# Skip term written into the accumulator bank, products in whole runs, and the third adding transfer one step later, in a fused Mamba, cross-attention and FFN kernel

## The chip, the cores and the metric

The kernel runs on one core of a Trainium2 chip. A core has a matrix engine (TensorE, PE in the tables; its weight loads are listed as PEld), a vector engine (VectorE, DVE), an activation engine (ScalarE, ACT), a general engine (GpSimd, POOL), a queue engine that issues transfers (SyncE, SP), 16 DMA engines, an on-chip memory of 128 partitions (SBUF) and eight accumulator banks (PSUM). The metric is the time of one execution in microseconds on the device.

## What is computed

Three residual blocks, each followed by a layer norm. Only the first is touched by the change.

```python
def _mamba(x, W_in, W_conv, b_conv, W_xproj, W_dt, b_dt, A_log, D, W_out):   # x: (8, 512, 512)
    xr = x @ W_in.T
    xc, res = (xr[..., :DI], xr[..., DI:])                     # DI = 1024
    u = silu(conv4(transpose(xc)) + b_conv)                    # causal, 4 taps, per channel
    x_dbl = jnp.einsum('bdl,ed->ble', u, W_xproj)              # -> dt (32), B (16), C (16)
    delta = jax.nn.softplus(dt @ W_dt.T + b_dt)
    A = -jnp.exp(A_log)
    dA = jnp.exp(jnp.einsum('bld,dn->lbdn', delta, A))         # 16 states per channel
    dBu = jnp.einsum('bld,bln,bdl->lbdn', delta, B, u)
    # h = dA_t * h + dBu_t ;  y_t = sum over the 16 states of h * C_t
    y = jnp.transpose(ys, (1, 2, 0)) + u * D[None, :, None]    # the skip term is u * D
    y = jnp.transpose(y, (0, 2, 1)) * silu(res)
    return y @ W_out.T

x = _layernorm(x + _mamba(x, ...))
x = _layernorm(x + cross_attention(x, ctx, ...))
x = _layernorm(x + ffn(x, ...))
```

## The kernel before

Two passes run one after the other. The first, `mamba_pass`, takes the first residual block; the second, `cross_attention_ffn_pass`, takes the other two and is the same text before and after.

The first pass walks over 64 blocks: 8 batches (b) times 8 groups of 128 channels (d). Below, g = 8b + d is the number of a block. In a block there are 8 steps, k = 0 to 7, each for two of the 16 states and all 512 time steps; q = 8g + k numbers the steps. Every engine has its own instruction stream, written out in program order as a loop over `step(b, d, k)`, and the streams meet only in semaphores. What each does in a step:

- PE, `b_products(q + 1)` (L381): sixteen small fp32 matmul instructions that make delta·u·B of the next step in one of two pairs of banks. It waits until the scan of step q − 1 has read the pair (`scanned`), so PE is at most two steps ahead of DVE.
- DVE, `scan` (L789): two scans, one per state, which turn the decays in a slot of a 12-slot ring into the states. Between scans it does the convolution taps (`conv_tap`, L765) of the next batch's u, the gating of y (`gate_y`, L797), and residual adds with layer norm statistics (`add_first`, L804; `add_second`, L811 to L816).
- ACT, `decay` (L635): two exponentials, which fill a ring slot some steps ahead of the scan. It waits until the slot's old content has been consumed. Between decays it takes results out of banks (`last_tap` L598, `take_vt` L619, `take_res` L643, `take_yt` L654) and computes silu and softplus, with a table load whenever the function set changes.
- POOL, `times_c` (L898): multiplies the states of a step by C. Three times a block it issues an adding transfer `merge(g, p)` (L907) of 1024 KB, which adds two ring slots onto the next two, so that after the third one only two slots of the block hold all the sums. Each of the three waits for the one before to have landed (`merged`).

In step k = 6 of the next block PE turns the two slots around into y's bank, adding them up (`state_sum`, L402). In between, four transposing matmuls (`skip_transposes`, L411) add u·D, which ACT had put into the buffer `y_t` in step k = 2 (`scale_skip`, L649). In step k = 7 ACT copies the bank into `y_t` (`take_yt`) and PE transposes it back into the same bank (`y_transposes`, L417), where DVE gates it.

The wide products, matmuls with 512 columns, stand between these in PE's stream. There are four families: `u_product` (L296, the convolution's input for the next batch), `x_product` (L306), `res_product` (L349), `out_first` and `out_second` (L436 and L444, the output projection). An fp32 product over one tile is two matmul instructions in the trace. A hand-written table says how many tiles of which product come in which step; most steps hold two tiles, which is half a `u_product` or `res_product`.

SP issues the loads. In the last block of a batch it fetches the next batch's rows of C (`mamba_c_row`, four times 1024 KB), B's diagonals (`mamba_diag_b`, eight times 256 KB) and an input tile (`mamba_xt`, 1024 KB).

Of the kernel before, what the change touches and what calls it, by code (L numbers as in the profile page):

```python
# [10 lines left out]
P = 128  # L11
# [3 lines left out]
def mamba_pass(nc, x, x_t, c_dram, diag_dram, w_u, w_res, w_conv, b_conv, w_x, w_dt, a_log, d_skip, w_out, ident_d, x1):  # L15
# [3 lines left out]
    KT = DM // P  # L19
# [24 lines left out]
    with ctx:  # L44
# [235 lines left out]
        def _(pe):  # L280
# [127 lines left out]
            def skip_transposes(g):  # L408
# [40 lines left out]
            def step(b, d, k):  # L449
# [25 lines left out]
                if d in (0, 4):  # L475
                    if k == 3:
                        res_product(g, [0, 1])
                    if k == 7:
                        res_product(g, [2, 3])
                if d in (1, 5, 7):  # L480
                    if k == 2:
                        res_product(g, [0, 1])
                    if k == 3:
                        res_product(g, [2, 3])
                if d in (2, 3):
                    if k == 3:
                        res_product(g, [0, 1])
                    if k == 4:
# [1166 lines left out]
```

## Time and profile before

| | |
|---|---|
| median of three runs | 2563.59 us |
| lowest, highest | 2558.22, 2564.44 us |
| the profiled execution's own time | 2562.99 us |
| its span, first to last instruction | 2561.2 us |
| mean granted TensorE clock, share of full speed | 0.973 |
| PE, PEld busy | 94%, 55% of the span |
| DVE, ACT, POOL busy | 71%, 58%, 65% of the span |

Busy shares are means over both passes. The first pass ends at about 1706 us of the span; the questions of this change are all asked there. A row of a timeline merges like instructions that follow each other and gives the start of the first; the difference between the starts of two rows of one engine is what the first cost, which is a little less than the busy time in the row, since instructions overlap at their ends. A bracket at the end of a row is idle time in front of it, and what ended it. "Issuing" a transfer on POOL has a row of its own.

### The profile page before, as it was taken

The page shows a single profiled execution, that of the slowest core. Times are in us where ns is not written, and L with a number is a line of the kernel's source. Part 1 is how long each engine was busy: PE and PEld are TensorE (multiplying, and loading weights), DVE is VectorE, ACT ScalarE, POOL GpSimd, SP SyncE. Part 2 cuts the span into 40 slices and gives each one's busy share as a digit, 9 for nine tenths or more (in the row PEclk, how much of TensorE's full clock was granted, in tenths as well). Part 3 has the DMA queues.
Part 4 walks back from the last instruction along what each step waited for, and adds up shares of the span by engine and source line. Part 5 has one row for each costly group of instructions (what it writes and reads, how often), then busy time and mean ns, then how long its engine had stood idle before and what let it go on. Part 6 is the DMA issues. An engine that isn't in the chain of part 4 may idle for free. (4 is left out here: it accounts for less than half of the span.)

```text
span 2561.2 us, 38451 instructions
## 1 busy us (share of the span) xinstructions
PE 2395.1 (94%) x15488; PEld 1418.2 (55%) x15488; DVE 1829.3 (71%) x2154; ACT 1473.8 (58%) x2258; POOL 1668.6 (65%) x912
## 2 busy tenths in 40 slices
PE   7899999999999999999999988877999999999997
PEld 3566566656665666656656656653545455454543
DVE  2898798798798789789879879841364565466453
ACT  2586678678678668768766867731333343443332
POOL 0698899798898889889978989860331332234130
PEclk8899999999999999999999999988999999999998
DMA  3777978978977887897897797755000100010000
GB/s 126 201 163 163 236 162 173 241 162 177 230 169 167 206 207 161 182 235 161 170 245 154 165 227 154 164 119 211 1 1 34 33 11 23 34 34 1 17 17 17
DMA packets 158832, 342.75 MB, mean 134 GB/s; under 512 B 39232, under 2 KB 102208, under 8 KB 127808
## 3 DMA queue, kind: packets, MB, share of 16 engines
q0 software_dynamic: 27648, 201.34, 40.0%
q1 hardware_dynamic: 131008, 138.97, 16.5%
q8 instruction: 123, 2.02, 0.3%
q14 instruction: 53, 0.43, 0.1%
HBM read 119.57 MB, written 19.37 MB: 54 GB/s over the span
## 5 line engine op out<-in xcount | busy, mean ns | idle before, releaser
L898 POOL TENSOR_TENSOR mamba_ring<-mamba_ring,mamba_c_row 128x1024 f32<-128x1024 f32 x512 | 1278.3, 2631 | 63.1 <-DVE mamba_ring L789 60.9
L789 DVE TENSOR_TENSOR_SCAN mamba_ring<-mamba_ring,ps 128x512 f32<-128x512 f32 x1024 | 1180.4, 1203 | 190.8 <-PE ps L381 190.0
L635 ACT ACTIVATE mamba_ring<-mamba_delta,mamba_a_neg 128x512 f32<-128x512 f32 x1024 | 661.2, 711 | 111.0 <-DMA mamba_ring<-mamba_ring 109.7
L381 PEld LDWEIGHTS ps<-mamba_diag_b,mamba_v_t 64*128 64x128 f32 x8192 | 504.7, 189 | 320.9 <-issue 244.3
L381 PE MATMUL ps<-mamba_diag_b,mamba_v_t 64*128 64x128 f32 x8192 | 595.5, 286 | 34.3 <-DVE mamba_ring L789 33.5
L296 PE MATMUL ps<-mamba_xt,mamba_wu 128*128 128x512 f32 x512 | 254.5, 625 | 31.7 <-DMA mamba_xt<-x_t 16.1
L907 POOL DMA_DIRECT2D mamba_ring<-mamba_ring x192 | 179.6, 936 | 142.0 <-DMA mamba_ring<-mamba_ring 107.4
L1554 POOL TENSOR_TENSOR xf_pr<-xf_pr,xf_top 128x1232 f32<-128x1232 f32 x32 | 75.0, 2343 | 281.0 <-DVE xf_top L1472 281.0
L349 PE MATMUL ps<-mamba_xt,mamba_wres 128*128 128x512 f32 x512 | 256.6, 619 | 0.0
L402 PE MATMUL ps<-mamba_ident,mamba_ring 128*128 128x128 f32 x1024 | 145.2, 288 | 43.7 <-DMA mamba_ring<-mamba_ring 43.6
L765 DVE SCALAR_TENSOR_TENSOR mamba_u<-ps,mamba_wcv,mamba_u 128x511 f32<-128x511 f32 (+2 forms) x192 | 142.4, 741 | 54.6 <-ACT mamba_u L598 50.9
L436 PE MATMUL ps<-mamba_wout,mamba_u 128*128 128x512 f32 x352 | 175.3, 617 | 0.0
L1547 POOL TENSOR_TENSOR xf_xn<-xf_xn,xf_bo_s 128x512 f32<-128x512 f32 x32 | 39.5, 1266 | 204.5 <-PE xf_ps L1122 204.5
L296 PEld LDWEIGHTS ps<-mamba_xt,mamba_wu 128*128 128x128 f32 x512 | 90.3, 194 | 115.4 <-issue 96.8
L402 PEld LDWEIGHTS ps<-mamba_ident,mamba_ring 128*128 128x128 f32 x1024 | 121.1, 148 | 52.1 <-issue 46.2
L598 ACT ACTIVATE mamba_u<-ps,mamba_bcv,mamba_wcv 128x512 f32<-128x512 f32 x64 | 49.5, 773 | 155.4 <-PE ps L296 155.4
L1335 ACT ACTIVATE xf_pr<-xf_pr 128x1232 f32<-128x1232 f32 x32 | 39.3, 1230 | 168.7 <-POOL xf_pr L1554 168.7
L1513 DVE TENSOR_TENSOR xf_xn<-xf_xn,xf_ps 128x512 f32<-128x512 f32 x32 | 21.2, 662 | 158.3 <-PE xf_ps L1231 158.3
L890 POOL TENSOR_TENSOR mamba_v<-mamba_delta,mamba_u 128x512 f32<-128x512 f32 x64 | 98.1, 1533 | 45.2 <-ACT mamba_delta L615 44.3
L1361 ACT COPY xf_pt<-xf_ps 77x512 f32<-77x512 f32 x128 | 64.8, 587 | 103.0 <-PE xf_ps L1214 103.0
L349 PEld LDWEIGHTS ps<-mamba_xt,mamba_wres 128*128 128x128 f32 x512 | 85.5, 189 | 69.0 <-issue 53.5
L586 ACT ACT_TABLE_LOAD x95 | 121.9, 1283 | 1.7
(116 smaller groups left out, 2948.6 us busy)
## 6 DMA issues: line engine op xcount, KB each, us to landing
mamba_ring<-mamba_ring POOLq DMA_DIRECT2D x192, 1024.0 KB, 7.8
mamba_c_row<-c_rows SPq DMA_DIRECT2D x32, 1024.0 KB, 15.7
mamba_wu<-w_u SPq DMA_DIRECT2D x64, 256.0 KB, 3.5
mamba_wres<-w_res SPq DMA_DIRECT2D x64, 256.0 KB, 6.0
mamba_diag_b<-b_diagonals SPq DMA_DIRECT2D x56, 256.0 KB, 14.9
mamba_xt<-x_t SPq DMA_DIRECT2D x8, 1024.0 KB, 16.0
mamba_xres<-x SPq DMA_DIRECT2D x32, 256.0 KB, 8.7
x<-mamba_xres SPq DMA_DIRECT2D x32, 256.0 KB, 5.8
```

The costliest lines, as they stand in the source:

```text
L296: m = nc.tensor.matmul(ps[:, bank, :], wu[n % 2][:, kt, :], xt[b % 2][:, kt, :], start=(kt == 0), stop=(kt == KT - 1))
L349: m = nc.tensor.matmul(ps[:, BANK_B, :], wres[g % 2][:, kt, :], xt[b % 2][:, kt, :], start=(kt == 0), stop=(kt == KT - 1))
L381: m = nc.tensor.matmul(ps[:, 2 * s + i, tb * P:(tb + 1) * P], v_t[g % 2][i * H:(i + 1) * H, tb * P:(tb + 1) * P], diag_b[i * H:(i + 1) * H ...
L402: m = nc.tensor.matmul(ps[:, y_bank(g), tb * P:(tb + 1) * P], ring[:, r, i, tb * P:(tb + 1) * P], ident[:], is_transpose=True, start=(k == ...
L436: m = nc.tensor.matmul(ps[:, o1_bank(tb), :], u[b % 2][:, d, tb * P:(tb + 1) * P], wout[:, d, :], start=(d == 0), stop=(d == MOST[tb] - 1))
L586: nc.scalar.preload_act_table_set("natural_log_exp_and_others")
L635: a = nc.scalar.activation(ring[:, q % NR, i, :], delta[:, d % EARLY, :], ACT.Exp, scale=a_neg[:, d, 2 * k + i:2 * k + i + 1])
L765: nc.vector.scalar_tensor_tensor(u[b % 2][:, j, lag:], ps[:, bank, 0:T - lag], wcv[:, j, TP - lag:TAPS - lag], u[b % 2][:, j, lag:], ALU.m ...
L789: m = nc.vector.tensor_tensor_scan(ring[:, r, i, :], ring[:, r, i, :], both[:, bass.ds(i, T, 2)], 0.0, ALU.mult, ALU.add)
L890: nc.gpsimd.tensor_tensor(v[:].rearrange("p b i t -> p i b t"), in_blocks(delta[:, d % EARLY, :]), in_blocks(u[b % 2][:, d, :]), ALU.mult) ...
L898: nc.gpsimd.tensor_tensor(ring[:, q % NR], ring[:, q % NR], c_row[:, 2 * k:2 * k + 2, :], ALU.mult).then_inc(c_done, 1)
L907: nc.gpsimd.dma_start(ring[:, dst:dst + 2], ring[:, src:src + 2], accum_op=ALU.add).then_inc(merged[p], 16)
```

## The change

Three things are done in the first pass.

First, the skip term goes another way. `skip_transposes` is gone from PE. ACT no longer writes u·D into `y_t` in step 2; in step 7, right after `take_yt` has copied y's bank out, it writes u·D into that same bank, and `y_transposes` adds onto it instead of overwriting. `y_transposes` now waits for both ACT instructions.

Second, wide products that stood in halves in neighbouring steps are put together, mostly four tiles in one step: `u_product` in steps 1 and 5, `res_product` in step 3 (5 where d = 6), `x_product` in steps 1 and 5 of d = 5, `out_first` and `out_second` in fewer, longer runs. Three residual adds on DVE move a step or two earlier with them.

Third, POOL issues the third adding transfer of a block behind the third `times_c` of the next block, where it stood behind the second.

```diff
+            def y_transposes(g):
+                pe.wait_ge(yt_ready, g + 1)
                 pe.wait_ge(du_ready, g + 1)
                 for tb in range(TT):
-                    nc.tensor.matmul(ps[:, y_bank(g), tb * P:(tb + 1) * P], y_t[:, tb * P:(tb + 1) * P], ident[:],
-                                     is_transpose=True, start=False, stop=False, skip_group_check=True)
-
-            def y_transposes(g):
-                pe.wait_ge(yt_ready, g + 1)
-                for tb in range(TT):
-                    m = nc.tensor.transpose(ps[:, y_bank(g), tb * P:(tb + 1) * P], y_t[:, tb * P:(tb + 1) * P],
-                                            ident[:])
+                    m = nc.tensor.matmul(ps[:, y_bank(g), tb * P:(tb + 1) * P], y_t[:, tb * P:(tb + 1) * P], ident[:],
+                                         is_transpose=True, start=False, stop=(tb == TT - 1), skip_group_check=True)
                 m.then_inc(y_back, 1)
...
                 if k == 6 and g >= 1:
-                    state_sum(g - 1, SUMS[0])
-                    skip_transposes(g - 1)
-                    state_sum(g - 1, SUMS[1])
+                    for e in SUMS:
+                        state_sum(g - 1, e)
...
-                    if k < 2:
-                        u_product(n, BANK_A, [2 * k, 2 * k + 1])
-                    if k in (4, 5) and d in TWO_U:
-                        u_product(n + 1, BANK_A, [2 * k - 8, 2 * k - 7])
+                    if k == 1:
+                        u_product(n, BANK_A, range(KT))
+                    if k == 5 and d in TWO_U:
+                        u_product(n + 1, BANK_A, range(KT))
...
-                    if k in (0, 1):
-                        x_product(b + 1, [2 * k, 2 * k + 1])
-                    if k in (4, 5):
-                        x_product(b + 1, [2 * k - 4, 2 * k - 3])
+                    if k in (1, 5):
+                        x_product(b + 1, range(k - 1, k + 3))
...
+                if k == (5 if d == 6 else 3):
+                    res_product(g, range(KT))
...
             def scale_skip(g):
                 b, d = g // ND, g % ND
+                act.wait_ge(yt_ready, g + 1)
+                nc.scalar.activation(ps[:, y_bank(g), :], u[b % 2][:, d, :], ACT.Copy,
+                                     scale=dsk[:, d:d + 1]).then_inc(du_ready, 1)
+
+            def take_yt(g):
+                act.wait_ge(summed, (g + 1) * NSUM)
                 if g >= 1:
                     act.wait_ge(y_back, g)
...
-                if k == 2 and g >= 1:
-                    scale_skip(g - 1)
                 if k == 7 and g >= 1:
                     take_yt(g - 1)
+                    scale_skip(g - 1)
...
-                if back and (d, k) == (3, 3):
+                if back and (d, k) == (3, 1):
                     add_second(b - 1, 2, y_bank(g - 1))
...
-                if (d, k) == (6, 4):
+                if (d, k) == (6, 3):
                     add_first(b, 0)
...
-                if (d, k) == (7, 5):
+                if (d, k) == (7, 3):
                     add_first(b, 2)
...
-                    if k == 1 and g >= 1:
+                    if k == 2 and g >= 1:
                         merge(g - 1, 2)
```

On PE, the front half of a block with d = 1 (from y's transposes of the block before to the small products of step 6), before. L296 is `u_product`, L349 `res_product`, L362 the transposes of v, L381 the small products of one step (x8 is one step here):

```order
L417 MATMUL ps<-mamba_ident,mamba_y_t 128x128 x4
L381 MATMUL ps<-mamba_diag_b,mamba_v_t 128x128 x8
L296 MATMUL ps<-mamba_xt,mamba_wu 128x512 x2
L381 MATMUL ps<-mamba_diag_b,mamba_v_t 128x128 x8
L296 MATMUL ps<-mamba_xt,mamba_wu 128x512 x2
L381 MATMUL ps<-mamba_diag_b,mamba_v_t 128x128 x8
L349 MATMUL ps<-mamba_xt,mamba_wres 128x512 x2
L381 MATMUL ps<-mamba_diag_b,mamba_v_t 128x128 x8
L349 MATMUL ps<-mamba_xt,mamba_wres 128x512 x2
L381 MATMUL ps<-mamba_diag_b,mamba_v_t 128x128 x8
L362 MATMUL ps<-mamba_ident,mamba_v 128x128 x4
L296 MATMUL ps<-mamba_xt,mamba_wu 128x512 x2
```

The same place after:

```order
L412 MATMUL ps<-mamba_ident,mamba_y_t 128x128 x4
L381 MATMUL ps<-mamba_diag_b,mamba_v_t 128x128 x16
L296 MATMUL ps<-mamba_xt,mamba_wu 128x512 x4
L381 MATMUL ps<-mamba_diag_b,mamba_v_t 128x128 x16
L349 MATMUL ps<-mamba_xt,mamba_wres 128x512 x4
L381 MATMUL ps<-mamba_diag_b,mamba_v_t 128x128 x8
L362 MATMUL ps<-mamba_ident,mamba_v 128x128 x4
L381 MATMUL ps<-mamba_diag_b,mamba_v_t 128x128 x8
L296 MATMUL ps<-mamba_xt,mamba_wu 128x512 x4
```

Where every step held two tiles, the small products of two steps now stand together and then come four tiles at once.

On ACT, from a block's `take_yt` to the u product's last tap in step 2 of the next block (d = 1), before. L649 is the skip term, L635 the decays, L643 the gate, L604 silu, L598 the last tap:

```order
L654 COPY mamba_y_t<-ps 128x512
L635 ACTIVATE mamba_ring<-mamba_delta,mamba_a_neg 128x512 x2
L643 ACT_TABLE_LOAD
L643 ACTIVATE mamba_gate<-ps 128x512
L604 ACTIVATE mamba_u<-mamba_u 128x512
L586 ACT_TABLE_LOAD
L635 ACTIVATE mamba_ring<-mamba_delta,mamba_a_neg 128x512 x4
L649 ACTIVATE mamba_y_t<-mamba_u,mamba_dsk 128x512
L598 ACTIVATE mamba_u<-ps,mamba_bcv,mamba_wcv 128x512
```

The same place after:

```order
L614 COPY mamba_y_t<-ps 128x512
L607 ACTIVATE ps<-mamba_u,mamba_dsk 128x512
L594 ACTIVATE mamba_ring<-mamba_delta,mamba_a_neg 128x512 x2
L602 ACT_TABLE_LOAD
L602 ACTIVATE mamba_gate<-ps 128x512
L563 ACTIVATE mamba_u<-mamba_u 128x512
L545 ACT_TABLE_LOAD
L594 ACTIVATE mamba_ring<-mamba_delta,mamba_a_neg 128x512 x4
L557 ACTIVATE mamba_u<-ps,mamba_bcv,mamba_wcv 128x512
```

The skip term has moved from in front of the last tap to right behind the copy out of y's bank, for which PE's last transposes of the block wait.

On POOL, one block and the start of the next, before. L890 makes v, L898 is `times_c`, L907 an adding transfer:

```order
L890 TENSOR_TENSOR mamba_v<-mamba_delta,mamba_u 128x2x4x64
L898 TENSOR_TENSOR mamba_ring<-mamba_ring,mamba_c_row 128x1024 x2
L907 DMA mamba_ring<-mamba_ring 128x2048
L898 TENSOR_TENSOR mamba_ring<-mamba_ring,mamba_c_row 128x1024 x2
L907 DMA mamba_ring<-mamba_ring 128x2048
L898 TENSOR_TENSOR mamba_ring<-mamba_ring,mamba_c_row 128x1024 x3
L907 DMA mamba_ring<-mamba_ring 128x2048
L898 TENSOR_TENSOR mamba_ring<-mamba_ring,mamba_c_row 128x1024
```

The same place after:

```order
L849 TENSOR_TENSOR mamba_v<-mamba_delta,mamba_u 128x2x4x64
L857 TENSOR_TENSOR mamba_ring<-mamba_ring,mamba_c_row 128x1024 x3
L866 DMA mamba_ring<-mamba_ring 128x2048
L857 TENSOR_TENSOR mamba_ring<-mamba_ring,mamba_c_row 128x1024
L866 DMA mamba_ring<-mamba_ring 128x2048
L857 TENSOR_TENSOR mamba_ring<-mamba_ring,mamba_c_row 128x1024 x3
L866 DMA mamba_ring<-mamba_ring 128x2048
L857 TENSOR_TENSOR mamba_ring<-mamba_ring,mamba_c_row 128x1024
```

Between the block before's third transfer and this block's first there were two C products, and now there is one.

## Rows read from the trace of the kernel before

**Rows 1.** Windows: busy us of each engine, granted clock, DMA share, GB/s.

```profile
core 0: us, PE busy (x) PEld busy (x) DVE busy (x) ACT busy (x) POOL busy (x), PEclk, DMA share, GB/s
868.00:922.00 54.00, 51.26 (x377) 31.95 (x376) 43.83 (x43) 35.06 (x51) 42.12 (x24) 1.00 1.02 266
...
900.00:1100.00 200.00, 195.27 (x1492) 123.34 (x1488) 174.12 (x179) 149.04 (x223) 173.67 (x94) 1.00 0.83 187
```

**Rows 2.** Timeline of PE, batch 4, blocks d = 0 to 2.

```profile
893.66 0.60 PE L417 MATMUL ps<-mamba_ident,mamba_y_t 128*128 128x128 f32 x4
...
896.52 1.98 PE L296 MATMUL ps<-mamba_xt,mamba_wu 128*128 128x512 f32 x4 [1.16 <-DMA mamba_xt<-x_t]
...
922.02 1.16 PE L381 MATMUL ps<-mamba_diag_b,mamba_v_t 64*128 64x128 f32 x16
923.11 1.98 PE L296 MATMUL ps<-mamba_xt,mamba_wu 128*128 128x512 f32 x4
925.02 1.16 PE L381 MATMUL ps<-mamba_diag_b,mamba_v_t 64*128 64x128 f32 x16
...
942.47 0.60 PE L411 MATMUL ps<-mamba_ident,mamba_y_t 128*128 128x128 f32 x4
942.90 1.04 PE L402 MATMUL ps<-mamba_ident,mamba_ring 128*128 128x128 f32 x8
...
962.90 2.84 PE L444 MATMUL ps<-mamba_wout,mamba_u 128*128 128x512 f32 x6
965.67 1.16 PE L381 MATMUL ps<-mamba_diag_b,mamba_v_t 64*128 64x128 f32 x16
...
1098.33 0.60 PE L417 MATMUL ps<-mamba_ident,mamba_y_t 128*128 128x128 f32 x4
```

**Rows 3.** Timeline of PE around waits: batches 4, 6, 2 and 7.

```profile
916.27 1.06 PE L402 MATMUL ps<-mamba_ident,mamba_ring 128*128 128x128 f32 x8 [1.57 <-DMA mamba_ring<-mamba_ring]
...
918.58 1.16 PE L381 MATMUL ps<-mamba_diag_b,mamba_v_t 64*128 64x128 f32 x16
...
1326.63 1.94 PE L402 MATMUL ps<-mamba_ident,mamba_ring 128*128 128x128 f32 x8 [2.67 <-DMA mamba_ring<-mamba_ring]
...
1330.50 1.16 PE L381 MATMUL ps<-mamba_diag_b,mamba_v_t 64*128 64x128 f32 x16
...
577.26 1.16 PE L381 MATMUL ps<-mamba_diag_b,mamba_v_t 64*128 64x128 f32 x16 [1.85 <-DVE mamba_ring L789]
...
1538.84 2.06 PE L381 MATMUL ps<-mamba_diag_b,mamba_v_t 64*128 64x128 f32 x32
```

**Rows 4.** Timeline of POOL, batch 4, blocks d = 0 and 1.

```profile
905.27 0.88 POOL L907 DMA_DIRECT2D mamba_ring<-mamba_ring  x1 [3.81 <-DMA mamba_ring<-mamba_ring]
905.88 4.97 POOL L898 TENSOR_TENSOR mamba_ring<-mamba_ring,mamba_c_row 128x1024 f32<-128x1024 f32 x2
911.15 0.88 POOL L907 DMA_DIRECT2D mamba_ring<-mamba_ring  x1 [0.30 <-POOL mamba_ring L898]
911.75 7.28 POOL L898 TENSOR_TENSOR mamba_ring<-mamba_ring,mamba_c_row 128x1024 f32<-128x1024 f32 x3
921.91 0.88 POOL L907 DMA_DIRECT2D mamba_ring<-mamba_ring  x1 [2.88 <-DMA mamba_ring<-mamba_ring]
922.52 2.66 POOL L898 TENSOR_TENSOR mamba_ring<-mamba_ring,mamba_c_row 128x1024 f32<-128x1024 f32 x1
924.84 1.57 POOL L890 TENSOR_TENSOR mamba_v<-mamba_delta,mamba_u 128x512 f32<-128x512 f32 x1
926.07 4.96 POOL L898 TENSOR_TENSOR mamba_ring<-mamba_ring,mamba_c_row 128x1024 f32<-128x1024 f32 x2
930.70 1.17 POOL L907 DMA_DIRECT2D mamba_ring<-mamba_ring  x1
```

**Rows 5.** Transfers: queue 0 over the span; L907 in 868 to 922; in 925 to 1040.

```profile
q0 software_dynamic: 27648, 201.34, 40.0%
...
mamba_ring<-mamba_ring POOLq DMA_DIRECT2D x6, 1024.0 KB, 11.2
...
mamba_ring<-mamba_ring POOLq DMA_DIRECT2D x14, 1024.0 KB, 7.6
```

**Rows 6.** Timeline of ACT: the hand-over of y, and the skip term.

```profile
918.69 0.58 ACT L654 COPY mamba_y_t<-ps 128x512 f32<-128x512 f32 x1
...
926.70 0.71 ACT L649 ACTIVATE mamba_y_t<-mamba_u,mamba_dsk 128x512 f32<-128x512 f32 x1
```

**Rows 7.** Timeline of DVE: three steps' scans in a row; two taps and the next scan.

```profile
903.22 1.53 DVE L765 SCALAR_TENSOR_TENSOR mamba_u<-ps,mamba_wcv,mamba_u 128x511 f32<-128x511 f32 x2 [0.38 <-ACT mamba_u L598]
904.67 2.32 DVE L789 TENSOR_TENSOR_SCAN mamba_ring<-mamba_ring,ps 128x512 f32<-128x512 f32 x2
...
907.55 6.76 DVE L789 TENSOR_TENSOR_SCAN mamba_ring<-mamba_ring,ps 128x512 f32<-128x512 f32 x6
```

More of the change, by code:

```diff
@@ L406, in state_sum @@
                 m.then_inc(summed, 1)
-            def skip_transposes(g):
+            def y_transposes(g):
+                pe.wait_ge(yt_ready, g + 1)
                 pe.wait_ge(du_ready, g + 1)
                 for tb in range(TT):
-                    nc.tensor.matmul(ps[:, y_bank(g), tb * P:(tb + 1) * P], y_t[:, tb * P:(tb + 1) * P], ident[:],
-                                     is_transpose=True, start=False, stop=False, skip_group_check=True)
-            def y_transposes(g):
-                pe.wait_ge(yt_ready, g + 1)
-                for tb in range(TT):
-                    m = nc.tensor.transpose(ps[:, y_bank(g), tb * P:(tb + 1) * P], y_t[:, tb * P:(tb + 1) * P],
-                                            ident[:])
+                    m = nc.tensor.matmul(ps[:, y_bank(g), tb * P:(tb + 1) * P], y_t[:, tb * P:(tb + 1) * P], ident[:],
+                                         is_transpose=True, start=False, stop=(tb == TT - 1), skip_group_check=True)
                 m.then_inc(y_back, 1)
@@ L500, in step @@
                 if d == 6:
-                    if k == 0:
-                        out_first(b, 0, [2, 3])
                     if k == 1:
-                        out_first(b, 1, [0, 1])
-                    if k == 2:
-                        out_first(b, 1, [2])
+                        out_first(b, 0, [2, 3, 4])
                     if k == 3:
-                        out_first(b, 0, [4])
-                        out_first(b, 1, [3])
-                    if k == 4:
-                        out_first(b, 1, [4])
+                        out_first(b, 1, [0, 1, 2, 3, 4])
+                    if k == 7:
+                        out_first(b, 2, [0, 1])
                 if d == 7:
-                    if k == 0:
-                        out_first(b, 2, [0, 1])
                     if k == 1:
-                        out_first(b, 2, [2, 3])
-                    if k == 4:
-                        out_first(b, 2, [4, 5])
+                        out_first(b, 2, [2, 3, 4, 5])
                     if k == 5:
-                        out_first(b, 3, [0, 1])
+                        out_first(b, 3, [0, 1, 2, 3])
                     if k == 7:
-                        out_first(b, 3, [2, 3, 4])
+                        out_first(b, 3, [4])
                 if back and (d, k) == (0, 0):
@@ L533, in step @@
                     dt_pair(b, 2)
-                if back and (d, k) == (1, 6):
+                if back and (d, k) == (1, 7):
                     pe.wait_ge(vt_ready, g + 2)
-                    out_second(b - 1, 0, y_bank(g), [5])
-                if back and (d, k) == (1, 7):
-                    out_second(b - 1, 0, y_bank(g), [6, 7])
+                    out_second(b - 1, 0, y_bank(g), [5, 6, 7])
                 if back and (d, k) == (2, 5):
@@ L545, in step @@
                     out_second(b - 1, 1, BANK_A, [5, 6, 7])
-                if back and (d, k) == (3, 2):
+                if back and (d, k) == (3, 0):
                     pe.wait_ge(vt_ready, g + 1)
@@ L574, in _ @@
                         step(b, d, k)
-            state_sum(NG - 1, SUMS[0])
-            skip_transposes(NG - 1)
-            state_sum(NG - 1, SUMS[1])
+            for k in SUMS:
+                state_sum(NG - 1, k)
             y_transposes(NG - 1)
@@ L646, in scale_skip @@
                 b, d = g // ND, g % ND
-                if g >= 1:
-                    act.wait_ge(y_back, g)
-                nc.scalar.activation(y_t[:], u[b % 2][:, d, :], ACT.Copy,
+                act.wait_ge(yt_ready, g + 1)
+                nc.scalar.activation(ps[:, y_bank(g), :], u[b % 2][:, d, :], ACT.Copy,
                                      scale=dsk[:, d:d + 1]).then_inc(du_ready, 1)
@@ L653, in take_yt @@
                 act.wait_ge(summed, (g + 1) * NSUM)
+                if g >= 1:
+                    act.wait_ge(y_back, g)
                 nc.scalar.copy(y_t[:], ps[:, y_bank(g), :]).then_inc(yt_ready, 1)
@@ L748, in _ @@
                         step(b, d, k)
+            take_yt(NG - 1)
             scale_skip(NG - 1)
-            take_yt(NG - 1)
             for tb in range(0, TT, 2):
```

22 lines of the change are left out of this document (removed).

## The prediction, made before the changed kernel had run

> **What bounds the kernel now.** I read four views in this order: the windows, the timeline of PE, the timeline of POOL, the transfers. The windows show the first pass: PE is busy for 195.27 of 200 us, DVE for 174.12, POOL's arithmetic for 173.67, and the DMA engines for 83% [rows 1]. So PE bounds it, but three others are close behind. At the turn from one batch to the next (868 to 922) the DMA engines are full, at 1.02 [rows 1].
>
> PE's timeline shows what filling it took. Step after step costs 3.0 us: the small products 1.09 (922.02 to 923.11), two tiles of a wide product 1.91 (923.11 to 925.02) [rows 2]. DVE's scans of a step cost 2.24 (6.76 for three, less 0.04 of overlap), and it can lag by at most two steps, so even steps of 3.0 leave room for taps in between. Batch 4 takes 204.67 us from y's transposes at 893.66 to the same at 1098.33, eight blocks [rows 2]; all of PE's idle gaps in it sum to 5.9 us, of which the two large kinds are a wait for the input tile (1.16) [rows 2] and one for an adding transfer (1.57) [rows 3]. PE's work per batch is then 204.7 − 5.9 = 198.8 us. The second pass does not change.
>
> I make the sum per batch, against batch 4, which has no stretch of low clock, and carry it to 2562.99 us, the profiled execution's own time. That stands 0.6 us below the median of the three runs, nothing beside the terms.
>
> **What the change takes from PE.** (a) The skip transposes: four per block, 942.47 to 942.90, 0.43 us [rows 2], times 8 = 3.5 per batch. (b) Run ends. Six wide instructions take 2.77 (962.90 to 965.67), four take 1.91 [rows 2], so one costs 0.43 and every run carries 1.91 − 4 × 0.43 = 0.19, say 0.2, once. Counted in the two tables, a batch has 54 such runs before and 30 after: 24 × 0.2 = 4.8. (c) Small products of two steps side by side: a pair is busy for 2.06 [rows 3] where two apart take 1.09 + 1.16 = 2.25. With some 8 such pairs per batch free of waits I take 1.4. Together 9.7, PE's work falls to 189.1 us. The input tile's wait goes too, since the first `u_product` now stands one step later than the 1.16 us that it waited. That is the case for the change: if PE stayed busy it would be worth 7% of the pass.
>
> **What it adds: (A) y's hand-over.** Before, two tiles or more stood between the sums and `y_transposes`. Now, in d = 0, 2, 3 and 4, only the small products of one step do, 1.09 us. In that time ACT must start (0.11 after the sums end: 918.58 to 918.69), copy (0.58) and write the skip term (0.71) [rows 3, 6], and the next engine must notice, 0.1: 1.5 us. PE waits 0.4. Where a second u product stands in step 5 (d = 0 and 4), ACT takes its last tap before the decays and comes out 0.2 later. 2 × 0.4 + 2 × 0.6 = 2.0 per batch. The trace has no ACT write from SBUF into a bank: the nearest rows are 0.58 (bank to SBUF) and 0.71 (SBUF to SBUF) [rows 6], so ±0.1 a block; I take 0.71, the same source and scale. What was behind ACT's skip term before, the last tap in step 2, gains 0.6.
>
> The Trainium skill, page ScalarE: Activation LUTs, section on the path of an ACTIVATE, says that ScalarE writes to PSUM faster than to SBUF. By it the 0.71 would shrink; even at the 0.58 row, (A) falls by 8 × 0.13 = 1.0 per batch at most. The trace has no row of that kind.
>
> **(B) Uneven steps.** With four tiles, a step takes 1.1 + 3.6 = 4.7 us and its neighbours 1.1. PE may be only two steps ahead of the scans, so it pays for the light ones. Worked for a block with two u products (times from its start): steps 0 and 1 begin at 0 and 1.1, the product ends at 5.8, the last tap is out 0.9 later, two taps 1.5, scan 3 ends at 10.4, a tap, scan 4 at 13.4; step 5's small products wait for scan 4. Its u product ends at 18.2, tap at 19.8, scan 7 ends at 22.1, two taps (1.45 [rows 7]) at 23.5, and the next block's scan 0 at 25.8. Where that block's k = 7 holds no wide product (d = 0, 4), PE is in the next block by 24 to 25.5, its second small products need scan 0, and PE waits 1.3. Going so through d = 0 to 7 I get waits of 1.0 in d = 1 (0.7 of it because ACT, with its gate and silu, is late for the last tap), 1.3 in d = 3 (the same), 1.6 in d = 4 (the add with statistics before it) and 1.3 in d = 5: 5.2 per batch. Bounds: 2 (DVE's lag is absorbed) and 8. The wait of this kind in d = 3 before, 1.85 [rows 3], goes.
>
> **(C) The adding transfers.** This is the term that decides. Each occupies all 16 engines for 40.0% × 2561.2 / 192 = 5.3 us [rows 5], and two in flight stand in line: the one issued at 905.27 lets PE go at 916.27 [rows 3], the next, 5.9 later at 911.15, lets POOL go at 921.9 [rows 4], 5.6 after the first, though alone one lands in 7.6 [rows 5]. Now the third transfer comes one C product later, 2.3 us or, at the scans' pace, up to 3, and the next block's first only 3.2 us behind it (0.6 + 2.3 + 0.3). So that one lands 5.5 after the third, some 9.5 to 10 after its own issue, and POOL waits for it before the second transfer. The wait at the third vanishes (3.81 in row 905.27) and reappears at the second (2.88 there already) [rows 4]. POOL's loop is then: third issued, 6.7 to land, 5.5 for the next, 1.1 to react, 0.6, four C products and v (4 × 2.32 + 1.23) = 24.7 us. A block is 25.6, so the lag hardly drains. POOL's stream alone, 8 × 2.32 + 1.23 + 3 × 0.9 = 22.5, would fit. Queued behind a waiting transfer are the C products of the block, for which decays and SP's loads of C rows wait.
>
> In d = 1 to 6 there is room: 4 to 5 us pass between landing and `state_sum`. At the turn of the batch, where a transfer takes 11.2 [rows 5], there is none: before, PE waited 1.57 in d = 0 and in batch 6 2.67 [rows 3]. There the third transfer of d = 6 is issued some 3 to 5 us later in d = 7, PE waits 3.5; the first of d = 7 stands behind it, POOL waits 6 us at the second instead of 2.9, and the third of d = 7 lands 3 us later: PE waits 4.2 in d = 0 and 0.7 in d = 1. Sum 8.4 per batch; bounds 2.4 (what batch 4 had) and 12.
>
> **(D) The clock.** Before, the granted clock falls to 1.2 GHz for a few us after gaps of PE: after the 1.85 at 577.26 in batch 2 and the 2.67 in batch 6, where the sums up to the next small products then take 3.87 (1326.63 to 1330.50) instead of 2.31 (916.27 to 918.58) [rows 3]. That is 1.56 a fall. With waits of 3.5 and 4.2 in each batch and some of 1.3 to 1.6, I take 2.5 falls, 3.9 us.
>
> **Sum.** 189.1 + 2.0 + 5.2 + 8.4 + 3.9 = 208.6 against 204.7, +3.9 for each of the six middle batches, 23.4. The first batch has no output products behind it and the last no u products and waits for transfers already: +1 each. 2562.99 + 25.4 = 2588 us.
>
> **The rivals.** (1) PE's savings hold: the transfers do not stand in line more than before, (C) stays at 2.4 and (D) at 1.6. Then 189.1 + 2.0 + 5.2 + 2.4 + 1.6 = 200.3, 4.4 less a batch, with 4 for the outer two 2533 us. For it: POOL is freed from its wait, 3.81 us in a row [rows 4]. Against: the 5.6 us spacing of two landings. It decides by whether the first transfer of a block lands before POOL's seventh C product. The Trainium skill, page DMA: Bandwidth & Descriptors, section on the anatomy of a SWDGE DMA, gives 2.0 us plus the bytes at 436 GB/s; an estimate by that page is 2.4 us of moving for 1024 KB, and two transfers 3.2 apart would not meet: this rival's time. The rows of this case, 7.6 and 5.3 us of all engines, are against it. (2) Gains and waits cancel: (B) 3, (C) 6, (D) 2.5 give 202.6, within 2 us a batch: 2553 to 2571, middle 2560. (3) Worse: POOL's lag grows through the batch and PE waits at the sums of d = 1 to 6 as well, 1 us each: 214.6 and 2625 us. For it: a loop of 24.7 beside blocks that I put at 23 to 26.
>
> That the change doesn't do what it says is excluded by PE's stream: the transposes are gone and the runs are whole.
>
> **Chances.** Slower as forecast 0.50, much slower 0.09, cancel 0.16, savings hold 0.25. A measurement of this kernel tells about 0.3% (7.7 us) from no change. Faster by more 0.26, within 0.15, slower by more 0.59. The range goes from rival 1 to rival 3: 2533 to 2625.
>
> **What would show it.** In the profile after: L411's successor gone and PE's small products in x32 rows; small gaps of 0.4 in front of L412 released by ACT (A); gaps of 1 to 2 us in front of L381 released by DVE (B); PE's wait for the ring transfer at `state_sum` 3 to 5 us in d = 7 and d = 0, and POOL's waits on its second transfer, hardly any on its third (C); a granted clock below 0.97 (D). I am wrong if POOL waits nowhere for its own transfers, or if PE's gaps per batch sum to less than 13.

## The result, and the profile after

The changed kernel takes 2613.43 us (median of four runs, 2611.23 to 2617.41) against 2561.34 us before. The ratio is 1.0197, with a 95% interval of 1.0178 to 1.0216: slower by 52 us. The prediction was 2588 us, slower, in a range of 2533 to 2625.

Below, from the page of the changed kernel: span, busy time by engine, and two groups of part 5 (busy us, mean ns of one, idle time in front and what ended it).

```profile
span 2612.5 us, 38066 instructions
...
PE 2354.6 (90%) x15232; PEld 1414.2 (54%) x15232; DVE 1813.9 (69%) x2154; ACT 1481.8 (57%) x2258; POOL 1666.5 (64%) x912
...
L866 POOL DMA_DIRECT2D mamba_ring<-mamba_ring x192 | 182.6, 951 | 233.8 <-DMA mamba_ring<-mamba_ring 205.8
...
L402 PE MATMUL ps<-mamba_ident,mamba_ring 128*128 128x128 f32 x1024 | 149.3, 308 | 111.8 <-DMA mamba_ring<-mamba_ring 111.3
```

The same two groups on the page of the kernel before:

```profile
L907 POOL DMA_DIRECT2D mamba_ring<-mamba_ring x192 | 179.6, 936 | 142.0 <-DMA mamba_ring<-mamba_ring 107.4
...
L402 PE MATMUL ps<-mamba_ident,mamba_ring 128*128 128x128 f32 x1024 | 145.2, 288 | 43.7 <-DMA mamba_ring<-mamba_ring 43.6
```

PE is busy 40 us less than before and the profiled span is 51 us longer. PE's idle time in front of the sums (L402) is 111.8 us; it was 43.7. POOL's in front of its own adding transfers is 233.8; it was 142.0.

The waits of PE and POOL between 300 and 1500 us of the span (below only "in 300 to 1500"), changed kernel (who waited for whom: us in total, times, longest):

```profile
PE ps L402 <- DMA mamba_ring<-mamba_ring: 65.5, 29, 5.5
PE ps L412 <- ACT ps L607: 17.8, 24, 1.2
PE ps L381 <- DVE mamba_ring L748: 15.0, 23, 1.2
PE ps L296 <- DMA mamba_xt<-x_t: 0.5, 1, 0.5
...
POOL mamba_ring L866 <- DMA mamba_ring<-mamba_ring: 148.0, 48, 7.4
```

The same of the kernel before:

```profile
PE ps L381 <- DVE mamba_ring L789: 13.8, 18, 1.9
PE ps L402 <- DMA mamba_ring<-mamba_ring: 11.1, 6, 2.7
PE ps L296 <- DMA mamba_xt<-x_t: 7.4, 5, 1.9
...
POOL mamba_ring L907 <- DMA mamba_ring<-mamba_ring: 70.6, 28, 4.8
```

What the waits for scans cost has hardly changed, the input tile's wait has gone, y's hand-over costs 17.8 us, and the transfers cost PE 54 us more.

By batches, counted from the first scan of one to the first scan of the next (the last one to its last scan), with PE's gaps summed by the instruction behind them. The rows between the lengths are us per batch, means of the six middle ones:

| | before | after |
|---|---|---|
| length of the six middle batches, mean | 205.5 | 210.8 |
| PE idle | 5.7 | 16.5 |
| of it at the sums | 2.1 | 10.9 |
| of it at y's transposes | 0 | 3.0 |
| of it at the small products (scans) | 2.3 | 2.5 |
| of it at the input tile | 1.2 | 0.1 |
| time at the lower clock (1.2 GHz) | 2.3 | 6.8 |
| first batch, length | 205.1 | 215.4 |
| last batch, length | 197.6 | 205.4 |

The mechanism can be followed in batch 4 of the changed kernel, block d = 5. Timeline of POOL and of PE, to be read beside [rows 4] and [rows 3]:

```profile
1061.56 1.16 POOL L866 DMA_DIRECT2D mamba_ring<-mamba_ring  x1
1062.17 2.94 POOL L857 TENSOR_TENSOR mamba_ring<-mamba_ring,mamba_c_row 128x1024 f32<-128x1024 f32 x1
1065.41 0.88 POOL L866 DMA_DIRECT2D mamba_ring<-mamba_ring  x1 [0.30 <-POOL mamba_ring L857]
1066.01 7.26 POOL L857 TENSOR_TENSOR mamba_ring<-mamba_ring,mamba_c_row 128x1024 f32<-128x1024 f32 x3
1076.60 0.88 POOL L866 DMA_DIRECT2D mamba_ring<-mamba_ring  x1 [3.33 <-DMA mamba_ring<-mamba_ring]
```

```profile
1066.13 1.16 PE L381 MATMUL ps<-mamba_diag_b,mamba_v_t 64*128 64x128 f32 x16
1071.19 3.30 PE L402 MATMUL ps<-mamba_ident,mamba_ring 128*128 128x128 f32 x16 [3.90 <-DMA mamba_ring<-mamba_ring]
1074.41 1.16 PE L381 MATMUL ps<-mamba_diag_b,mamba_v_t 64*128 64x128 f32 x16
```

The third transfer (1061.56) and the first of the next block (1065.41) are now 3.85 us apart. PE waits 3.90 us for the third, and its sums then take 3.22 us (1071.19 to 1074.41) at a granted clock of 0.57; at 1.00 they take 1.87 (941.57 to 943.44 in the same batch). POOL waits 3.33 us for the first at its second transfer (1076.60), and all its later work waits with it.

y's hand-over, batch 4, d = 0, on PE and ACT, beside [rows 6]:

```profile
943.44 1.16 PE L381 MATMUL ps<-mamba_diag_b,mamba_v_t 64*128 64x128 f32 x16
945.42 0.63 PE L412 MATMUL ps<-mamba_ident,mamba_y_t 128*128 128x128 f32 x4 [0.82 <-ACT ps L607]
...
941.52 2.56 ACT L594 ACTIVATE mamba_ring<-mamba_delta,mamba_a_neg 128x512 f32<-128x512 f32 x4 [1.97 <-DMA mamba_ring<-mamba_ring]
943.99 0.56 ACT L614 COPY mamba_y_t<-ps 128x512 f32<-128x512 f32 x1
944.58 0.69 ACT L607 ACTIVATE ps<-mamba_u,mamba_dsk 128x512 f32<-128x512 f32 x1
```

ACT is still at the decays, which started when the transfer landed, as PE did; then it copies and writes. PE waits 0.82 us.

### The profile page after: what moved, and what is told of

Same layout as the page of the kernel before. It is cut to its first block and busy times, and to the rows that moved or that the text cites. A ratio compares the mean times of both kernels' runs of the same rounds, so it can differ in the third digit from the quotient of the medians.

```text
span 2612.5 us, 38066 instructions
## 1 busy us (share of the span) xinstructions
PE 2354.6 (90%) x15232; PEld 1414.2 (54%) x15232; DVE 1813.9 (69%) x2154; ACT 1481.8 (57%) x2258; POOL 1666.5 (64%) x912
## 5 line engine op out<-in xcount | busy, mean ns | idle before, releaser
L857 POOL TENSOR_TENSOR mamba_ring<-mamba_ring,mamba_c_row 128x1024 f32<-128x1024 f32 x512 | 1277.2, 2648 | 24.7 <-DVE mamba_ring L748 23.8
L381 PEld LDWEIGHTS ps<-mamba_diag_b,mamba_v_t 64*128 64x128 f32 x8192 | 504.9, 190 | 241.2 <-issue 141.9
L381 PE MATMUL ps<-mamba_diag_b,mamba_v_t 64*128 64x128 f32 x8192 | 586.2, 286 | 49.7 <-DVE mamba_ring L748 48.8
L866 POOL DMA_DIRECT2D mamba_ring<-mamba_ring x192 | 182.6, 951 | 233.8 <-DMA mamba_ring<-mamba_ring 205.8
L296 PE MATMUL ps<-mamba_xt,mamba_wu 128*128 128x512 f32 x512 | 242.8, 620 | 17.9 <-DMA mamba_xt<-x_t 9.3
L402 PE MATMUL ps<-mamba_ident,mamba_ring 128*128 128x128 f32 x1024 | 149.3, 308 | 111.8 <-DMA mamba_ring<-mamba_ring 111.3
L349 PE MATMUL ps<-mamba_xt,mamba_wres 128*128 128x512 f32 x512 | 237.7, 607 | 0.0
L402 PEld LDWEIGHTS ps<-mamba_ident,mamba_ring 128*128 128x128 f32 x1024 | 133.2, 160 | 121.2 <-issue 118.2
L431 PE MATMUL ps<-mamba_wout,mamba_u 128*128 128x512 f32 x352 | 168.8, 613 | 0.0
L296 PEld LDWEIGHTS ps<-mamba_xt,mamba_wu 128*128 128x128 f32 x512 | 95.5, 196 | 125.1 <-issue 117.6
L349 PEld LDWEIGHTS ps<-mamba_xt,mamba_wres 128*128 128x128 f32 x512 | 92.3, 190 | 100.3 <-issue 92.6
```

Source lines behind the costliest of these rows:

```text
L296: m = nc.tensor.matmul(ps[:, bank, :], wu[n % 2][:, kt, :], xt[b % 2][:, kt, :], start=(kt == 0), stop=(kt == KT - 1))
L349: m = nc.tensor.matmul(ps[:, BANK_B, :], wres[g % 2][:, kt, :], xt[b % 2][:, kt, :], start=(kt == 0), stop=(kt == KT - 1))
L381: m = nc.tensor.matmul(ps[:, 2 * s + i, tb * P:(tb + 1) * P], v_t[g % 2][i * H:(i + 1) * H, tb * P:(tb + 1) * P], diag_b[i * H:(i + 1) * H ...
L402: m = nc.tensor.matmul(ps[:, y_bank(g), tb * P:(tb + 1) * P], ring[:, r, i, tb * P:(tb + 1) * P], ident[:], is_transpose=True, start=(k == ...
L431: m = nc.tensor.matmul(ps[:, o1_bank(tb), :], u[b % 2][:, d, tb * P:(tb + 1) * P], wout[:, d, :], start=(d == 0), stop=(d == MOST[tb] - 1))
L857: nc.gpsimd.tensor_tensor(ring[:, q % NR], ring[:, q % NR], c_row[:, 2 * k:2 * k + 2, :], ALU.mult).then_inc(c_done, 1)
```

## The experiments

Twelve kernels were run, each against runs of the kernel before on the same chip.

### Which part of the change costs

Four kernels with one or two of the three parts.

The transfer alone:

```diff
-                    if k == 1 and g >= 1:
+                    if k == 2 and g >= 1:
                         merge(g - 1, 2)
```

> The kernel before with one edit: POOL issues the third adding transfer behind the third C product of the next block. Theory 1 (transfers in line: the third transfer of a block and the first of the next, now 3.2 us apart, stand in one line, POOL waits at the second and PE at the sums): the loss is here already, 4 to 6 us a batch, 2590 to 2610 us, with POOL idle in front of its transfers more than the 70.6 us of before in 300 to 1500. Theory 2 (the loss comes from the uneven steps that the whole runs make, the transfer's place is harmless since 4 to 5 us lay between landing and sums): 2561 to 2568 us.

Measured: 2611.75 us, ratio 1.0196 (1.0178 to 1.0215). One line costs all that the whole change costs, 1.75 us beyond the top of theory 1's range. POOL's wait at its transfers is 125.0 us in 300 to 1500, PE's at the sums 40.5:

```profile
POOL mamba_ring L907 <- DMA mamba_ring<-mamba_ring: 125.0, 42, 8.2
...
PE ps L402 <- DMA mamba_ring<-mamba_ring: 40.5, 14, 7.6
PE ps L381 <- DVE mamba_ring L789: 13.8, 18, 1.9
```

Here most of PE's wait is in d = 7, 6.4 of 7.6 us a batch. In batch 4:

```profile
1123.22 1.94 PE L402 MATMUL ps<-mamba_ident,mamba_ring 128*128 128x128 f32 x8 [6.00 <-DMA mamba_ring<-mamba_ring]
1124.95 1.06 PE L411 MATMUL ps<-mamba_ident,mamba_y_t 128*128 128x128 f32 x4
1125.81 1.91 PE L402 MATMUL ps<-mamba_ident,mamba_ring 128*128 128x128 f32 x8
1127.65 1.80 PE L381 MATMUL ps<-mamba_diag_b,mamba_v_t 64*128 64x128 f32 x16
```

After a wait of 6 us the sums and skip transposes take 4.43 us at a granted clock of 0.50, instead of 2.31 [rows 3]: the lower clock adds 2.1.

The runs alone (the edits of the diff in the wide products and the three adds):

```diff
-                    if k < 2:
-                        u_product(n, BANK_A, [2 * k, 2 * k + 1])
+                    if k == 1:
+                        u_product(n, BANK_A, range(KT))
...
+                if k == (5 if d == 6 else 3):
+                    res_product(g, range(KT))
```

> The kernel before with one edit: the wide products in whole runs (with the three residual adds that move with them); skip term and transfers as before. Theory 1: 24 run ends less per batch at 0.2 us and the waits for scans that uneven steps bring nearly cancel or leave a gain: 2535 to 2562 us. Theory 2: the uneven steps starve DVE and make PE wait for scans: 2585 to 2610 us.

Measured: 2554.69 us, ratio 0.9977 (0.9960 to 0.9995). A small gain: PE's waits for scans rise from 2.3 to 4.6 us a batch, which takes back most of what the run ends saved, and theory 2 falls.

The skip term alone:

```diff
                 if k == 7 and g >= 1:
                     take_yt(g - 1)
+                    scale_skip(g - 1)
...
-                    skip_transposes(g - 1)
```

> The kernel before with one edit: the skip term written by ACT into y's bank behind the copy, no skip transposes. In each block at least one wide tile stands in step 7 in front of y's transposes, so ACT's 1.5 us are covered. Theory 1: PE loses 0.43 us of work 64 times and gains no wait: 27 us less, 2532 to 2545 us. Theory 2 (ACT's longer hand-over costs what the transposes saved): 2555 to 2570 us, with PE idle in front of y's transposes.

Measured: 2546.23 us, ratio 0.9943 (0.9923 to 0.9963), 16.6 us less: a gain, but 10 short of theory 1's 27 and 1 us outside its range. In the middle batches PE waits nowhere at y's transposes, so the hand-over is covered as expected. Of the 3.5 us taken from PE per batch 1.0 comes back as other waits (6.7 us idle against 5.7), and PE spends 3.4 us a batch at the lower clock against 2.3.

Skip and runs together, that is the changed kernel with its third part undone (`k == 1` again):

> The changed kernel with its third part undone: the third adding transfer stays behind the second C product. Theory 1: without the line of transfers the other two parts gain, what is left are waits of 0.4 to 0.8 us in front of y's transposes: 2525 to 2560 us, and PE's idle time in front of the sums falls from 10.9 to under 5 us a batch. Theory 2: still slow, 2590 to 2613 us.

Measured: 2546.52 us, ratio 0.9942 (0.9925 to 0.9958). PE's idle time at the sums is 3.3 us a batch. Undoing one line gives back 67 us. It also shows that the two parts don't add up: with both, PE waits 2.6 us a batch at y's transposes, since the runs took away the tiles in step 7 that covered ACT. The runs are worth nothing once the skip term has moved.

### Why one C product later costs 49 us

Transfers that stand in line can be seen in the packets of queue 0; a transfer's landing is here the end of its last packet. Medians over 300 to 1500, for the first transfer of a block: in the kernel before, it is issued 6.17 us behind the third of the preceding block and lands 6.55 behind it, 7.5 after its own issue. In the transfer-only kernel it is issued 3.87 behind and lands 5.50 behind, 9.2 after its issue; in the changed kernel 3.84, 5.71 and 9.7. So its landing does not keep pace with its issue, as expected. Two readings were left, called theory A and theory B in the expectations: POOL's wait for it, in a loop that goes round once per block, or the plain lateness of the third transfer where the DMA engines are full, at the turn of the batch.

```diff
-                    if k in (3, 6):
+                    if k in (3, 7):
                         merge(g, k // 4)
```

> The transfer-only kernel (third transfer behind the third C product, else as before) with the block's second transfer issued behind the eighth C product instead of the seventh, so that POOL multiplies where it waited. In the transfer-only kernel POOL waits 134 us for the first transfer in 300 to 1500. Theory A (POOL's wait in the loop makes the loss, by its lag): the wait falls under 60 us and the time comes back to 2560 to 2580 us. Theory B (what costs is that the third transfer itself leaves one C product later at the batch's turn, where PE has no room): POOL's wait falls all the same, but PE's wait at the sums in d = 7 stays at 5 us or more and the time at 2595 to 2612 us.

Measured: 2562.57 us, ratio 0.9993 (0.9981 to 1.0004). The whole 49 us are back with the third transfer as late as in the transfer-only kernel. POOL's waits in 300 to 1500:

```profile
POOL mamba_ring L898 <- DVE mamba_ring L789: 87.4, 95, 5.0
POOL mamba_ring L907 <- DMA mamba_ring<-mamba_ring: 27.5, 18, 2.5
```

POOL now waits for DVE's scans, as an engine with room does, and PE's wait in d = 7 is 0.1 us a batch. The later second transfer alone, with the third where it was before, was not run.

```diff
-                    if k == 2 and g >= 1:
+                    if k == (1 if g % ND in (0, ND - 1) else 2) and g >= 1:
                         merge(g - 1, 2)
```

> The transfer-only kernel, but in the last and the first block of a batch (d = 7 and d = 0) POOL issues the third transfer behind the second C product, as before; in the six others behind the third. Theory B (the loss sits at the batch's turn): 2560 to 2572 us, PE's wait at the sums of d = 7 falls from 6.4 us a batch to under 1. Theory A (the line of transfers in every block adds up to a lag that the turn only shows): at least a third of the loss stays, 2580 us or more.

Measured: 2611.42 us, ratio 1.0186 (1.0171 to 1.0202). Nothing is recovered. POOL waits no less than in the transfer-only kernel (125.0):

```profile
POOL mamba_ring L907 <- DMA mamba_ring<-mamba_ring: 144.7, 49, 6.7
```

PE's wait at the sums of d = 7 falls to 2.0 us a batch, but d = 5 rises from 0.8 to 2.0 and d = 0 from 0.1 to 1.5. Theory B has fallen.

To take load off the DMA engines at the turn, the next two kernels leave out all loads of C rows for batches 1 to 7. All their batches compute with the C of the first, so the two are to be compared with each other. The cut shows one of the two loads taken out; the waits for them go too.

```diff
                             load_diag(b + 1, p + 4)
-                            load_c(b + 1, p)
```

> The transfer-only kernel without the loads of C rows for batches 1 to 7 (4 x 1024 KB at each turn left out; all batches use the C of the first, so a part of the input of the computation is left out). To be read against the kernel before with the same left out. If the full DMA engines at the turn turn one late C product into PE's wait, the difference between the two falls from 49 to under 15 us and PE waits under 1.5 us a batch in d = 7. If the line of two adding transfers costs by itself, 25 us or more of the difference stays.

> The kernel before without the loads of C rows for batches 1 to 7 (same part left out). The waits at the turn (2 us at the sums of d = 0, 1.2 for the input tile) should go: 2535 to 2558 us.

Measured: 2598.46 and 2527.45 us, 71 us apart, more than with the loads. The waits of POOL and PE, first with the third transfer late, then before:

```profile
POOL mamba_ring L905 <- DMA mamba_ring<-mamba_ring: 133.0, 43, 7.2
...
PE ps L400 <- DMA mamba_ring<-mamba_ring: 40.9, 21, 5.7
PE ps L379 <- DVE mamba_ring L787: 13.8, 18, 1.9
```

```profile
POOL mamba_ring L905 <- DMA mamba_ring<-mamba_ring: 45.8, 20, 5.0
...
PE ps L379 <- DVE mamba_ring L787: 15.8, 21, 1.9
```

Without the C loads the kernel before has no wait at the sums left; with the third transfer late 40.9 us stay. The loads at the turn are not what makes one C product dear. They do cost 37 us by themselves in the kernel before (2564.02 on this chip to 2527.45), more than the 5 to 28 that I expected.

```diff
-                    if k in (3, 6):
-                        merge(g, k // 4)
+                    if k in (4, 6):
+                        merge(g, (k - 4) // 2)
```

> The transfer-only kernel with the block's first transfer behind the fifth C product instead of the fourth, so that it is again some 6 us behind the third of the block before. If transfers stand in a line, it lands no earlier or later than in the transfer-only kernel (5.3 to 6 us behind the one before), POOL waits as long for it at the second transfer (100 to 150 us in 300 to 1500) and the time stays at 2600 to 2615 us. If the short distance of the two issues itself is the trouble (two transfers disturbing each other), spacing them mends it: under 2575 us.

Measured: 2644.26 us, ratio 1.0331 (1.0310 to 1.0351), slower still, and outside what I expected for either case. The first transfer is issued 5.22 us behind the third and lands 6.92 behind it. POOL's wait in 300 to 1500:

```profile
POOL mamba_ring L907 <- DMA mamba_ring<-mamba_ring: 174.4, 45, 8.6
```

Spacing mends nothing. But my case was also incomplete: it is not the line alone that counts, it is when the first lands against when POOL gets to the second, and here only two C products lie between.

Four of these kernels can be set beside one loop on POOL, worked out from the median spacings and durations. From third to third: the time to the first transfer's issue, its duration, 1.0 to react, 0.6 for the second's issue, and what POOL does until the next third. Beside it, the three issue spacings (third to first, first to second, second to third) as measured, medians added up.

| kernel | loop | us | spacings measured | median time |
|---|---|---|---|---|
| before | 6.2 to the first, 8.7 to the second, then 7.4 + 1.0 until that has landed | 23.3 | 24.2 | 2563 |
| second behind the last C | 4.1 + 8.9 + 1.0 + 0.6 + three C and v 8.2 | 22.8 | 25.1 | 2563 |
| transfer only | 3.9 + 9.2 + 1.0 + 0.6 + four C and v 10.5 | 25.2 | 25.1 | 2612 |
| first behind the fifth C | 5.2 + 8.8 + 1.0 + 0.6 + 10.5 | 26.1 | 26.1 | 2644 |

In the last two kernels POOL takes just what the loop takes, in the first two it has room. The middle blocks of the kernel before last 25.7 us on average, but those with d = 2 and 4 only 24.4 and 23.6 (means of the six middle batches). A loop above that leaves POOL behind in such blocks, first transfers that take 12 us in d = 5 of the transfer-only kernel add to it, and the third transfer of d = 4 or 6 comes too late for PE. What I can show is the order of the four, the place of the waits, and that the time comes back when POOL no longer waits at the second transfer. That the loop's length sets the price is argued, not shown, and two results do not follow from it: with the longer loop in only six of eight blocks the loss is the same (2611.42), and without the C loads much the same lengthening costs 71 us instead of 49.

```diff
 (the changed kernel)
-                    if k in (3, 6):
+                    if k in (3, 7):
                         merge(g, k // 4)
```

> The changed kernel with the block's second transfer issued behind the eighth C product instead of the seventh. Alone, this edit brought the transfer-only kernel from 2611.75 to 2562.57 us. If POOL's wait for the first transfer is all that the changed kernel loses by, it comes down to the level of the kernel with the other two parts alone (2546.52 us): 2540 to 2553 us. If the uneven steps need the third transfer's time as well (PE's wait at the sums of d = 5 was 4.3 us a batch), it stays at 2565 us or above.

Measured: 2545.89 us, ratio 0.9942 (0.9928 to 0.9957). The changed kernel with this line is 68 us faster than without it and equal to the one with skip and runs alone. Its uneven steps did not need the third transfer's time. What is left of PE's waits in 300 to 1500:

```profile
PE ps L381 <- DVE mamba_ring L748: 20.3, 31, 1.1
PE ps L402 <- DMA mamba_ring<-mamba_ring: 19.8, 10, 2.8
PE ps L412 <- ACT ps L607: 14.0, 21, 1.2
```

### A version that beats both

From the single parts: the skip term in y's bank, the old halves in step 7 that cover it, and of the runs only the block d = 3.

```diff
-                    if k < 2:
+                    if d == 3:
+                        if k == 1:
+                            u_product(n, BANK_A, range(KT))
+                    elif k < 2:
                         u_product(n, BANK_A, [2 * k, 2 * k + 1])
...
-                if back and (d, k) == (3, 2):
+                if back and (d, k) == (3, 0):
```

> A candidate: the kernel before with the skip term in y's bank, and of the runs only what removes the waits in d = 3 (u product whole in step 1, output product in step 0, its add in step 1). In the two single-part kernels the mean d = 3 block took 26.4 us (skip only) and 24.8 (skip and runs), the d = 4 block 23.2 and 25.2. Expected 1.5 us less a batch than skip only, minus some in d = 4: 2530 to 2540 us.

Measured: 2549.08 us, ratio 0.9958 (0.9945 to 0.9971): a miss, no better than the skip term alone. The mean d = 3 block did fall from 26.4 to 24.8 us and d = 4 stayed at 23.0. The gain was lost again at the turn: PE waits 5.0 us a batch at the sums against 2.6 with the skip term alone, all of the rise in d = 6, 7 and 0. So I added the two edits on POOL, the third transfer behind the third C product and the second behind the eighth:

> The candidate with both the third transfer behind the third C product and the second behind the eighth. Over the kernel before, these two together gave 0.9993 (0.9981 to 1.0004): no difference from the candidate without them, 2528 to 2545 us. If POOL's place matters once PE is faster, 5 us or more less.

Measured: 2537.49 us, ratio 0.9904 (0.9887 to 0.9921), 24 us faster than before and the fastest of the kernels that compute the whole. The pair of edits was worth nothing on the kernel before and about 12 us here. POOL's wait for its transfers in 300 to 1500 fell from 96.7 to 59.5 us, but PE's wait at the sums did not, first without and then with the pair:

```profile
PE ps L402 <- DMA mamba_ring<-mamba_ring: 27.9, 15, 4.4
```

```profile
PE ps L402 <- DMA mamba_ring<-mamba_ring: 27.2, 18, 3.2
```

Nearly half of the gain is in the first batch (203.9 to 198.2 us), where PE's wait at the sums falls from 6.8 to 2.1. That PE has less to do here is not enough of a reason: on the kernel with skip term and runs, which leaves PE less work too, the same pair was worth nothing (2546.52 to 2545.89). Why it pays here is open.

## Why the prediction was right, and where it was off

**Direction and the deciding term.** I said slower, and that (C) decides. It does: the transfer's edit alone gives 2611.75 us, and undoing it gives 2546.52. The steps of (C) hold in the trace: the first transfer lands 5.5 to 5.7 us behind the third (predicted 5.5), 9.2 to 9.7 after its own issue (9.5 to 10); POOL's idle time in front of the third transfer goes and that in front of the second grows (summed over 300 to 1500: at the third 24.5 us before and 5.9 after, at the second 60.3 and 149.7), so most of it is new and not moved. Per middle batch PE waits 10.9 us at the sums; the term said 8.4, with bounds of 2.4 and 12.

**Where (C) was placed wrongly.** I put 7.7 of 8.4 us into d = 7 and 0 and gave the full DMA engines there as the reason. In the changed kernel d = 5 has 4.3, d = 0 2.1, d = 7 1.3 and d = 1 to 4 another 3.3. The experiments with the third transfer early at the turn and without the C loads show that the turn is not needed. The loop, which I had put at 24.7 (its terms add up to 24.4; 25.1 was measured with the transfer alone) and then treated as a side matter ("the lag hardly drains"), is where the cause lies: with POOL's wait at the second transfer out of it, the loss is gone. That is my third rival, lag that grows through the batch and waits in d = 1 to 6 as well, to which I gave 0.09. In these blocks PE waits 7.5 of the 10.9 us, and 2613 is nearer to its 2625 than to my 2588. The direction was reached by the line of transfers that I named, the place of the loss was not.

**The outer batches.** This is the step that is furthest off, 16 of the 25 us between 2588 and 2613. I gave the first and the last batch +1 us each; they are 10.3 and 7.8 longer. In the first, PE's waits for scans rise from 6.4 to 15.2 us and those at the sums from 3.9 to 12.0, while those for the input tile and the weights fall from 9.8 to 2.6; in the last, waits for scans rise from 13.4 to 18.8 and those at the sums from 16.0 to 21.0. In the kernel with skip and runs alone the two batches last 205.5 and 194.7, so the transfer's place costs some 10 us in each. The reason I gave for the last, that it waits for transfers already, was a reason for the opposite: its blocks are the shortest (24.7 us on average, 21.6 to 29.5), so a POOL loop of 25 us should weigh most there. That is argued from the lengths.

**The middle batches.** Six times 5.3 = 31.9 us, predicted 23.4. This is nearer than the terms are, since their errors cancel in part. Beside the prediction, PE's work is 1.8 us above, (A) 1.0 and (C) 2.5 above, (B) 2.7 below and (D) 0.5 below.

**(A), y's hand-over.** Predicted 2.0 us a batch, measured 3.0. All the waits are in the four blocks that I named, d = 0, 2, 3 and 4, and in each of their 24 blocks there is one; the mechanism held. What was too small is the size, 0.2 to 1.2 us each where I took 0.4 and 0.6: where PE has waited for the landing, the decays of the step start with it too, and ACT starts the copy 0.55 us after the sums in the row above (943.44 to 943.99) instead of 0.11. ACT's write into the bank has a mean of 691 ns over 64, the one into SBUF before had 709. The Trainium skill, page ScalarE: Activation LUTs, section Step-by-step: what each stage is for, says that a write to PSUM is the faster; the rows agree in sign, by 0.02 us.

**(B), uneven steps.** Predicted 5.2 a batch, measured 2.5 in the changed kernel and 4.6 with the runs alone. With skip term and runs together it was 3.4. That DVE catches up while PE waits elsewhere, so that the terms do not add, would explain the order of the three; no run shows it by itself. I had counted both terms in full.

**(D), the clock.** Predicted 2.5 falls a batch and 3.9 us. In the six middle batches the clock fell ten times (four times before), 1.7 a batch, and PE spent 6.8 us a batch at the lower clock, half of which, 3.4, is lost. I took 1.56 us a fall; the sums behind a wait of 3.90 cost 1.35 more than at full clock, those behind 6.00 cost 2.1 more.

**PE's work.** Predicted 189.1 us a batch after the savings. Length less idle time less half of the time at the lower clock is 210.8 − 16.5 − 3.4 = 190.9, before 205.5 − 5.7 − 1.2 = 198.6 (predicted 198.8). The savings are real, 7.7 of the 9.7 us: the skip term alone saves 3.4 (predicted 3.5), the runs alone 3.9 (predicted 6.2). The kernels without the transfer's edit show what they bring: 16 us in all.

**The rivals.** That the savings hold (2533) would have been nearest for a change without the third part: 2546.52. The estimate by the Trainium skill, page DMA: Bandwidth & Descriptors, section Anatomy of one DMA, by which two transfers 3.2 us apart would not meet, is against the landings in the trace here: issued 3.84 us apart they land 5.71 apart. The middle of rival 2, 2560, did not follow from its own sum: 202.6 us a batch, 2.1 less than before, gives about 2552. Rival 3 is answered above.

## What to carry to other kernels

A chain of transfers that one engine issues and waits for is a loop through that engine's other work. Before moving one link, add up the loop from issue to the same issue in the next round, with the time that a transfer takes in line and not alone (9.2 us here instead of 7.5), and compare it with the shortest rounds and not only with the mean; that the shortest decide is argued here, not shown. When such a wait stands in front of work that doesn't need it, move the waiting instruction behind that work: one C product in front of the wait instead of behind it was worth 49 to 68 us, more than the 16 us that all the savings on the busiest engine brought.

## What was not expected of the hardware

Two adding transfers of 1024 KB issued 3.9 us apart land 5.5 to 5.7 us apart and 9.2 to 9.7 after the second one's issue; issued 6.2 apart they land 6.6 apart, 7.5 after. That much was expected. Unexpected was that the same pair of edits on POOL is worth nothing on two kernels (2564 to 2563 us, 2547 to 2546) and 12 us on a third, and that the C loads, 28 transfers of 1024 KB in all, cost 37 us of a kernel whose DMA engines are 83% busy in the first pass.
